# A top-one routed feed-forward stage: from all experts on all tokens to tiles of tokens sorted by expert

## The chip, the cores and the metric

The kernel runs on 1 core of one Trainium2 chip. The metric is the device time of a run in microseconds; shown is the median of three runs.

## What is computed

Eight residual stages in a row on x of 4 x 512 tokens of 128 features, all in f32. Each stage is `x = x + f(layernorm(x))`. The change is to the fourth, a routed feed-forward of 8 experts with 256 hidden features each, of which every token uses one, and a shared expert that every token uses:

```python
logits = x_ @ router.T
idx = jnp.argmax(logits, axis=-1)
onehot = jax.nn.one_hot(idx, router.shape[0], dtype=x.dtype)
u = jnp.einsum('bc,ehc->ebh', x_, up)
g = jnp.einsum('bc,ehc->ebh', x_, gate)
h = jax.nn.silu(g) * u
ye = jnp.einsum('ebh,ech->ebc', h, down)
y = jnp.einsum('ebc,be->bc', ye, onehot)
ys = jax.nn.silu(x_ @ w_gate_s.T) * (x_ @ w_up_s.T) @ w_down_s.T
```

The second stage is of the same kind with 16 experts of 64 features, four of them used by a token. The last one has 8 experts of 512 features, two used by a token, with a limit on the tokens of an expert.

## The kernel before

x stays in SBUF from the first stage to the last (`x_resid`, 16 tiles of 128 tokens). `program` (L2999) runs the stages one after the other; each is a block with an order of its own for every engine, and all engines meet at its end. Two weight buffers (`wbuf`) alternate: `load_next` (L132) clears the semaphores of the stage before last and has SP load the next stage's weights during the present one.

The second and the fourth stage are both `routed_ffn` (L1139). It takes 4 groups of 512 tokens. For each it normalizes (`LayerNorm`: statistics and scaling on VectorE, L190 to L201, the power on GpSimd, L225, turns on TensorE, L235, copies on ScalarE, L247 and L251), makes logits (L1239) and, from the ranks of the scores (`route_top1`, L1084), a matrix of weights per token and expert, zero where an expert isn't chosen. Then it goes through units of 128 hidden features, 18 a group in the fourth stage: 2 of the shared expert and 16 of the experts. `gate_up` (L1242) makes the gate and up products of all 512 tokens in three matmuls each, since operands are split into a high and a low part (fp32r) made by ScalarE and GpSimd, and a product that spreads the expert's weight over the unit's rows (L1263). ScalarE does SiLU (L1354) and the high part of the hidden values (L1338), VectorE two products (L1408, L1411), GpSimd the low part (L1227). `down` (L1277) adds the unit's share to the output, three units later (`LAG`). At the end of a group the output is turned back (L1297) and added to x (L1379). In all, 72 units.

The last stage, `dispatched_ffn` (L2641), isn't changed, but has the same steps as the new code. It chooses experts per 512 tokens, counts with triangular and all-ones matmuls how many tokens ahead chose the same expert (L2796 to L2801), makes a row number for each token and choice (L2913), and GpSimd scatters rows of 129 numbers (128 features and the token's own number) into a DRAM buffer with one indirect DMA per 128 rows (L2757). SP reads the rows expert by expert (L2730), TensorE turns them (L2818), multiplies them in f32 (L2827, L2837), GpSimd scatters results by token (L2772), SP reads them back (L2736) and VectorE adds them to x (L2992). The fields of that buffer are cleared ahead, in the sixth stage (L1465, L1467).

## Time and profile before

| what | us |
| --- | --- |
| median of three runs | 1818.81 (1815.47 to 1820.68) |
| profiled execution, from its first to its last instruction | 1817.4 |
| TensorE busy in it (matmuls) | 1503.1 (83%) |
| VectorE | 1168.3 (64%) |
| ScalarE | 819.9 (45%) |
| GpSimd | 813.0 (45%) |
| the fourth stage, from 564.7 to 762.5: TensorE busy | 184.35 of 197.80 |

The profile is of one execution, of which only the span is known, and that is the time it is read against. Matmuls are pipelined and the ends of their records are modelled, so a row's length is more than its beat. "Busy" leaves out register, semaphore and DMA-issuing instructions. PEclk is the granted TensorE clock as a share of full speed (2.4 GHz): 0.50 is 1.2 GHz. In a row of the timeline, "[idle before <-releaser]" is how long the engine waited and for what.

### The profile page before, as it was taken

How to read it: one execution, taken by the hardware profiler on the slowest of the kernel's cores; microseconds unless marked ns; L12 is line 12 of the kernel's file. 1: busy time of each engine (PE TensorE's matmuls, PEld its weight loads, DVE VectorE, ACT ScalarE, POOL GpSimd, SP SyncE). 2: the span in 40 equal slices, each digit the busy share in tenths (PEclk: the TensorE clock that was granted, in tenths of full speed). 3: DMA queues.
4: the chain of work that ended last, by engine and by line, in shares of the span. 5: the costliest groups of instructions: out<-in, count | busy, mean ns of one | idle time of the engine just before them, and what ended most of it. 6: DMA issues, size and time to landing. Idle time of an engine off the chain costs nothing. (4 is left out here: it accounts for less than half of the span.)

```text
span 1817.4 us, 25752 instructions
## 1 busy us (share of the span) xinstructions
PE 1503.1 (83%) x9316; PEld 932.3 (51%) x9316; DVE 1168.3 (64%) x2949; ACT 819.9 (45%) x1276; POOL 813.0 (45%) x847
## 2 busy tenths in 40 slices
PE   5576677889997999769997889979999999986194
PEld 2355555544444677534443567754555554544063
DVE  5766688568884766678885332257877877675302
ACT  3544333336664554355664433345545545450041
POOL 5451344612223855562323254235546556463633
PEclk9687699759997999858999899989999999998597
DMA  2000000100000000210000102000000000002113
GB/s 90 7 7 2 32 0 1 79 1 1 1 1 23 1 1 1 81 51 1 1 1 1 38 11 94 1 1 1 1 1 1 1 1 1 1 1 109 60 53 93
DMA packets 21597, 38.66 MB, mean 21 GB/s; under 512 B 2016, under 2 KB 18400, under 8 KB 20320
## 3 DMA queue, kind: packets, MB, share of 16 engines
q1 hardware_dynamic: 19424, 32.81, 5.2%
q0 software_dynamic: 2048, 4.21, 0.7%
q8 instruction: 75, 1.23, 0.3%
q14 instruction: 50, 0.41, 0.1%
HBM read 26.50 MB, written 9.47 MB: 20 GB/s over the span
## 5 line engine op out<-in xcount | busy, mean ns | idle before, releaser
L1982 DVE CUSTOM_DVE_ANT_0 s_masked_scores<-s_for_max,s_mask_qk 128x128 bf16<-128x128 f32 (+3 forms) x512 | 227.0, 486 | 58.9 <-PE s_for_max L1806 56.9
L2415 POOL TENSOR_TENSOR wbuf<-s_probs 128x1024 f32<-128x1024 f32 x64 | 151.9, 2374 | 206.6 <-ACT s_probs L2574 206.6
L2574 ACT ACTIVATE s_probs<-s_scores 128x1024 f32<-128x1024 f32 x128 | 132.2, 1033 | 201.7 <-PE s_scores L2496 201.7
L1758 POOL TENSOR_SCALAR_AFFINE_SELECT s_probs<-s_probs 128x256 f32<-128x256 f32 x256 | 100.9, 406 | 269.2 <-ACT s_probs L1913 156.1
L1227 POOL TENSOR_TENSOR s_hidden_lo<-s_hidden,s_hidden_hi 128x512 fp32r<-128x512 f32 x108 | 142.6, 1321 | 122.0 <-ACT s_hidden_hi L1338 121.9
L2616 DVE TENSOR_REDUCE s_negmax<-s_for_max 128x2 f32<-128x1024 f32 x126 | 152.2, 1208 | 20.1 <-PE s_for_max L2471 20.0
L1806 PE MATMUL s_for_max<-s_k_stack,s_q_stack 32*128 32x128 f32 (+3 forms) x512 | 142.2, 441 | 27.1 <-DVE s_max_wide L1982 17.4
L2623 DVE RECIPROCAL s_recip<-s_pv_and_sums 128x128 f32<-128x128 f32 x128 | 116.7, 934 | 47.3 <-PE s_pv_and_sums L2522 47.3
L1806 PEld LDWEIGHTS s_for_max<-s_k_stack,s_q_stack 32*128 32x128 f32 x512 | 72.0, 204 | 129.4 <-DVE s_max_wide L1982 88.5
L1913 ACT ACTIVATE s_probs<-s_scores 128x1024 f32<-128x1024 f32 x128 | 127.3, 1024 | 17.1 <-PE s_scores L1827 17.0
L2509 PE MATMUL s_pv_and_sums<-s_probs,s_v 128*64 128x512 f32 x512 | 123.9, 605 | 0.9 <-DVE wbuf L2631 0.9
L1354 ACT ACTIVATE s_silu<-s_gate 128x512 f32<-128x512 f32 x108 | 64.5, 598 | 120.4 <-PE s_comb L1263 111.2
L1408 DVE TENSOR_TENSOR s_gated<-s_silu,s_up 128x512 f32<-128x512 f32 x96 | 65.9, 687 | 61.4 <-ACT s_silu L1354 60.5
L1900 ACT ACTIVATE s_low_rows_hi<-s_odd_jobs,s_low_rows_bias,s_low_rows 128x512 fp32r<-128x512 f32 x64 | 49.8, 777 | 102.9 <-PE s_odd_jobs L1786 102.1
L1841 PE MATMUL s_pv<-s_probs,s_v_and_one 128*32 128x512 f32 (+3 forms) x1024 | 94.2, 462 | 1.5 <-DVE s_o L2001 1.5
L1827 PE MATMUL s_scores<-s_q_stack,s_k_stack 32*128 32x512 f32 (+3 forms) x512 | 82.0, 396 | 0.7 <-ACT s_probs L1913 0.7
L2420 POOL TENSOR_TENSOR xnT<-wbuf 128x1024 f32<-128x1024 f32 x32 | 78.1, 2440 | 2.5
L1338 ACT CAST s_hidden_hi<-s_hidden 128x512 fp32r<-128x512 f32 x108 | 66.2, 613 | 22.0 <-DVE s_hidden L1411 21.9
L1489 POOL TENSOR_TENSOR s_h_lo<-s_h,s_h_hi 128x512 fp32r<-128x512 f32 x32 | 42.5, 1330 | 71.0 <-DVE s_h_hi L1583 71.0
L2496 PE MATMUL s_scores<-s_q_hi,s_k_hi 64*128 64x512 f32 x256 | 63.8, 494 | 9.6 <-ACT s_probs L2574 9.6
L1411 DVE TENSOR_TENSOR s_hidden<-s_gated,s_comb 128x512 f32<-128x512 f32 x96 | 65.9, 687 | 3.3
L1288 PE MATMUL s_yT<-s_hidden_hi,s_w_hi 128*128 128x512 f32 x108 | 61.0, 565 | 3.6 <-POOL s_hidden_lo L1227 3.6
(490 smaller groups left out, 3768.5 us busy)
## 6 DMA issues: line engine op xcount, KB each, us to landing
s_w<-extra SPq DMA_DIRECT2D x2, 2048.0 KB, 10.2
wbuf<-w SPq DMA_DIRECT2D x1, 3460.0 KB, 11.2
s_probs<-extra SPq DMA_DIRECT2D x1, 2898.0 KB, 9.7
wbuf<-w SPq DMA_DIRECT2D x1, 2888.0 KB, 15.2
wbuf<-w SPq DMA_DIRECT2D x1, 2124.0 KB, 8.3
dispatched<-s_empty_slots SPq DMA_DIRECT2D x1, 2064.0 KB, 6.6
s_rows<-dispatched SPq DMA_DIRECT2D x8, 258.0 KB
expert_rows<-s_empty_slots SPq DMA_DIRECT2D x1, 2048.0 KB, 14.7
```

Source lines behind the costliest of these rows:

```text
L1227: nc.gpsimd.tensor_tensor(hid_lo[:, n % DEEP, :], hidden[:, n % DEEP, :], hid_hi[:, n % DEEP, :].bitcast(F32), ALU.subtract).then_inc(s_lo, 1)
L1758: last = nc.gpsimd.affine_select(out=diag, in_=diag, compare_op=ALU.is_ge, fill=0.0, base=0, pattern=[[0, diag.shape[1]], [1, P]], channel ...
L1806: last = nc.tensor.matmul(p1[m % 2][:, at:at + n], stacks[0][rows, q % SLOTS, i * P:n], stacks[1][rows, q % SLOTS, 0:n], start=True, stop= ...
L1827: last = nc.tensor.matmul(p2[n % 2][:, at:at + S - j * P], stacks[1][rows, q % SLOTS, j * P:(j + 1) * P], stacks[0][rows, q % SLOTS, j * P ...
L1841: last = nc.tensor.matmul(po[32 * x:32 * x + 32, j * P:S], v32[:, c % 2, j, 4 * g + x, :], probs[:, q % 2, slab, at:at + S - j * P], start ...
L1913: nc.scalar.activation(probs[:, q % 2, r, :], p2[n % 2][:, :], ACT.Exp, scale=scale).then_inc(s_exp, 1)
L1982: last = nc.vector.tensor_tensor_reduce(out=junk[:, m % 2, at:at + n], in0=p1[m % 2][:, at:at + n], in1=mask[:, S - n:S], scale=1.0, scala ...
L2415: nc.gpsimd.tensor_tensor(added[half], probs[:, g % 2, 2 * half, :, :], probs[:, g % 2, 2 * half + 1, :, :], ALU.add).then_inc(s_added, 1)
L2509: last = nc.tensor.matmul(po[x * dh:(x + 1) * dh, :], v[:, c % 2, j, (2 * n + x) * dh:(2 * n + x + 1) * dh], probs[:, g % 2, j, x, :], sta ...
L2574: nc.scalar.activation(probs[:, g % 2, j, :, :], p2[:, :, :], ACT.Exp, scale=dh ** -0.5).then_inc(s_exp, 1)
L2616: nc.vector.tensor_reduce(negmax[:, g % 2, :, j], max_bank(g, j)[:, :, :], AX.X, ALU.max, negate=True).then_inc(s_neg, 1)
L2623: nc.vector.reciprocal(recip[:, at], ps_sum[:, at]).then_inc(s_rec, 1)
```

## The change

The fourth stage becomes a function of its own, `sorted_ffn`, and `route_top1` and its steps are gone. It finds the expert of each token, counts the tokens of each expert, and gives each token a row in a DRAM buffer in which expert e starts at row 2048 e. From the counts it makes a table of 23 tiles of 128 rows (16 would do for full ones; each of 8 experts can end in a part-filled tile): the first row of each tile and the place of its expert's weights. SP reads the first row numbers into registers and loads the tiles; TensorE reads the places into registers and uses them as addresses of the moving operand. The last column of a row is its token, or 1000000 where the field is empty; the result of an empty row goes to a spare row. Matmuls are in plain f32, with no split. Weights are laid out expert by expert. The buffer's fields are filled in the second stage.

```diff
+SORT_TILES = T // P + 7
+SORT_ROWS = 8 * T + 1024
+SORT_CLEARS = 9
+NO_TOKEN = 1.0e6
```

In `routed_ffn`, for the run of it that comes before (a stage 3 follows):

```diff
         def _(sp):
             sh.load_next(sp, stage)
+            if clear:
+                sp.wait_ge(s_empty, 2)
+                for at in range(0, SORT_ROWS, T):
+                    n = min(T, SORT_ROWS - at) // P
+                    sp.dma_start(sh.by_expert[at:at + n * P].rearrange("(p r) d -> p r d", p=P),
+                                 empty[:, 0:n, :]).then_inc(sh.fields_cleared, 16)
+                sp.wait_ge(sh.fields_cleared, 16 * SORT_CLEARS)
...
                     split.gpsimd(pool, range(3 * block_no, 3 * block_no + 3))
+                if n == units and clear:
+                    nc.gpsimd.memset(empty[:, :, 0:D], 0.0).then_inc(s_empty, 1)
+                    nc.gpsimd.memset(empty[:, :, D], NO_TOKEN).then_inc(s_empty, 1)
                 pool.wait_ge(s_hi, n + 1)
```

The new stage, engine by engine (J = 23, RING = 6, WIDE = 768 columns of weights an expert; the increments of semaphores are mostly left out):

```python
def _(sp):
    sh.load_next(sp, stage)
    sp.wait_ge(s_table, 1)
    _, at = nc.values_load_multi_w_load_instructions(table_i[0:1, 1, :], ...)
    sp.wait_ge(s_put, 16 * NT)
    for j in range(J):
        if j >= RING:
            sp.wait_ge(s_turn, j - RING + 1)
            sp.wait_ge(s_placed, j - RING + 1)
        sp.dma_start(rows[:, j % RING, :], sh.by_expert[bass.ds(at[j], P), :])
    sp.wait_ge(s_out, 16 * J)
    for c in range(B):
        sp.dma_start(back[:, tiles(c), :], ...)

def _(pool):
...
    pool.wait_ge(sh.fields_cleared, 16 * SORT_CLEARS)
    for c in range(B):
        pool.wait_ge(s_idx, c + 1)
        for t in range(c * TPC, (c + 1) * TPC):
            nc.gpsimd.indirect_dma_start(sh.by_expert, ...idx[:, t:t + 1]..., xn[:, t, :], None)
    for j in range(J):
        pool.wait_ge(s_placed, j + 1)
        pool.wait_ge(s_y, j + 1)
        nc.gpsimd.indirect_dma_start(sh.by_token, ...place_i[:, j:j + 1]..., y[:, j, :], None)

def _(pe):
...
    def shared_up(c, f):
        pe.wait_ge(ln.ready, c + 1)
        if c:
            pe.wait_ge(s_hid, (c - 1) * n_sh + f + 1)
        for m, ps in zip(("gate", "up"), (ps_gu, ps_h)[f]):
            last = nc.tensor.matmul(ps[:, :], w[m][:, f * P:(f + 1) * P], sh.xnT[:, cols(c)], start=True, stop=True)
...
    for c in range(2):
        ln.turned(pe, c)
        logits(c)
    count(0)
    shared_up(0, 0)
    pe.wait_ge(s_chosen, 1)
    ln.turned(pe, 2)
    logits(2)
    count(1)
    shared_up(0, 1)
    pe.wait_ge(s_chosen, 2)
    ln.turned(pe, 3)
    logits(3)
    count(2)
    shared_up(1, 0)
    count(3)
    shared_down(0)
    shared_up(1, 1)
    shared_down(1)
    for c in range(2, B):
        for f in range(n_sh):
            shared_up(c, f)
        shared_down(c)
    pe.wait_ge(s_table, 1)
    _, at = nc.values_load_multi_w_load_instructions(table_i[0:1, 0, :], ...)

    def gate_up(j):
        pe.wait_ge(s_rowsT, j + 1)
        pe.wait_ge(*((s_hide, j - 1) if j >= 2 else (s_hid, B * n_sh)))
        nc.tensor.matmul(ps_gu[j % 2][:, :], rowsT[:, j % 3, :], w["experts"][:, bass.ds(at[j], 2 * f_exp)],
                         start=True, stop=True).then_inc(s_gu, 1)
...
    def down(j):
        pe.wait_ge(s_hidT, j + 1)
...
        for f in range(n_f):
            w_f = w["experts"][:, 2 * f_exp + f * P:]
            last = nc.tensor.matmul(ps_out[j % 2][:, 0:D], hidT[:, j % 2, f * P:(f + 1) * P],
                                    w_f[:, bass.ds(at[j], D)], start=(f == 0), stop=(f == n_f - 1))
...
    turn(0)
    turn(1)
    for j in range(J + 2):
        if j < J:
            gate_up(j)
        if j + 2 < J:
            turn(j + 2)
        if j >= 2:
            down(j - 2)
        if 1 <= j <= J:
            turn_hidden(j - 1)

def _(act):
...
    for j in range(J + 2):
        if j < J:
            act.wait_ge(s_gu, j + 1)
            nc.scalar.activation(silu_e[:, j % 2, :], ps_gu[j % 2][:, 0:f_exp], ACT.Silu)
        if j + 2 < J:
            take_rows(j + 2)
        if j >= 2:
            act.wait_ge(s_down, j - 1)
            nc.scalar.copy(y[:, j - 2, :], ps_out[j % 2][:, 0:D])

def _(dve):
...
    for j in range(J + 1):
        if j < J:
            dve.wait_ge(s_rows[j % RING], 16 * (j // RING + 1))
            nc.vector.tensor_tensor(place_i[:, j:j + 1], rows[:, j % RING, D:D + 1], spare[:, j:j + 1], ALU.min)
            dve.wait_ge(s_esilu, j + 1)
            if j >= 2:
                dve.wait_ge(s_hturn, j - 1)
            nc.vector.tensor_tensor(hid_e[:, j % 2, :], silu_e[:, j % 2, :], ps_gu[j % 2][:, f_exp:], ALU.mult)
        if j >= 1:
            dve.wait_ge(s_hturn, j)
            if j >= 3:
                dve.wait_ge(s_down, j - 2)
            nc.vector.tensor_copy(hidT[:, (j - 1) % 2, :], ps_h[(j - 1) % 2][:, 0:f_exp])
    for c in range(B):
        dve.wait_ge(s_back[c], 16)
        nc.vector.tensor_tensor(sh.x[:, tiles(c), :], sh.x[:, tiles(c), :], back[:, tiles(c), :], ALU.add)
```

VectorE's part ahead of these loops chooses the expert of a group of 512 tokens in five small operations, gives rows in five more, and after the fourth group makes the table in twelve; the shared expert's products stand in between, two of them ahead of the table.

## Rows read from the trace of the kernel before

**Rows 1.** The page's head.

```profile
span 1817.4 us, 25752 instructions
```

**Rows 2.** Windows, fourth stage: from:to, length, busy us (instructions) of each engine, PEclk, DMA share, GB/s.

```profile
564.70:762.50 197.80, 184.35 (x792) 136.21 (x792) 129.51 (x238) 97.96 (x190) 119.22 (x113) 0.95 0.02 6
```

**Rows 3.** Windows, two stretches of the fourth stage; columns as in rows 2.

```profile
582.00:591.00 9.00, 9.00 (x36) 7.71 (x36) 1.55 (x3) 4.42 (x9) 2.20 (x4) 0.50 0.01 2
591.00:757.50 166.50, 163.66 (x716) 119.99 (x714) 112.80 (x173) 86.29 (x166) 104.35 (x90) 1.00 0.00 1
```

**Rows 4.** Timeline, fourth stage: start us, length us, engine, line, operation, out<-in, count.

```profile
751.10 0.39 PE L1254 MATMUL s_gate<-s_xnT_hi,s_w_hi 128*128 128x512 f32 x1
...
753.42 0.39 PE L1254 MATMUL s_gate<-s_xnT_hi,s_w_hi 128*128 128x512 f32 x1
...
761.68 0.69 DVE L1379 TENSOR_TENSOR x_resid<-x_resid,s_route 128x512 f32<-128x512 f32 x1 [4.39 <-PE s_route L1297]
...
762.66 0.13 POOL L1727 IOTA s_row_number<- 128x1 int32 x1 [3.37 <-POOLq L1152]
```

**Rows 5.** Timeline, second stage: GpSimd's tenth low part, and the last addition.

```profile
264.72 1.29 POOL L1227 TENSOR_TENSOR s_hidden_lo<-s_hidden,s_hidden_hi 128x512 fp32r<-128x512 f32 x1 [1.15 <-ACT s_hidden_hi L1338]
...
341.74 0.69 DVE L1379 TENSOR_TENSOR x_resid<-x_resid,s_route 128x512 f32<-128x512 f32 x1 [4.39 <-PE s_route L1297]
```

**Rows 6.** DMA issues: out<-in, engine, count, KB each, median us to landing.

```profile
expert_rows<-s_empty_slots SPq DMA_DIRECT2D x1, 2048.0 KB, 14.7
...
wbuf<-w SPq DMA_DIRECT2D x1, 20.0 KB, 1.7
```

**Rows 7.** Timeline, last stage: statistics, first and last indices, last scatter, read, turn.

```profile
1661.72 0.87 DVE L190 BATCH_NORM_STATS2 s_ln_stats<-x_resid 128x6 f32<-128x128 f32 x4 [0.32 <-PEq L2314]
...
1675.36 0.17 DVE L2913 CAST s_idx<-s_where 128x4 uint32<-128x4 f32 x1
...
1695.14 0.17 DVE L2913 CAST s_idx<-s_where 128x4 uint32<-128x4 f32 x1
...
1719.69 0.96 POOL L2757 DMA_INDIRECT dispatched<-s_xn,s_idx  x1 [0.30 <-issue]
...
1721.97 44.16 SPq L2730 DMA_DIRECT2D s_rows<-dispatched  x8
...
1724.80 1.12 PE L2818 MATMUL s_turned<-ident,s_rows 128*128 128x128 f32 x4 [31.30 <-DMA s_rows<-dispatched]
```

**Rows 8.** Groups by line, last stage: busy us, mean ns of one, idle before.

```profile
L2865 ACT COPY s_rowsT<-s_turned 128x512 f32<-128x512 f32 x8 | 4.6, 578 | 36.2 <-PE s_turned L2818 36.2
...
L307 DVE TENSOR_REDUCE s_rank<-s_gt 128x32 f32<-128x256 f32 x4 | 1.7, 420 | 0.1
```

**Rows 9.** Timeline, last stage, TensorE in the first and third expert.

```profile
1726.69 5.96 PE L2827 MATMUL s_up<-s_rowsT,s_w 128*128 128x512 f32 x8 [0.77 <-ACT s_rowsT L2865]
...
1741.63 3.79 PE L2827 MATMUL s_up<-s_rowsT,s_w 128*128 128x512 f32 x8
...
1745.25 0.60 PE L2818 MATMUL s_turned<-ident,s_rows 128*128 128x128 f32 x4
...
1745.69 3.74 PE L2837 MATMUL s_y<-s_w,s_hidden 128*128 128x128 f32 x32
```

**Rows 10.** SP's semaphore clears: ns min/median/max, first and last start.

```profile
L136 SPq EVENT_SEMAPHORE_RANGE_CLEAR  x277: 25/30/49, 203.9 to 1663.6; - x139
```

**Rows 11.** Timeline, end of the last stage: last scatter, reads back, additions.

```profile
1797.47 0.95 POOL L2772 DMA_INDIRECT expert_rows<-s_y,s_place_int  x1 [0.30 <-issue]
1799.76 5.52 SPq L2736 DMA_DIRECT2D s_back<-expert_rows  x8
1802.61 2.19 DVE L2992 SCALAR_TENSOR_TENSOR x_resid<-s_back,s_gate,x_resid 128x128 f32<-128x128 f32 x8 [11.16 <-DMA s_back<-expert_rows]
1805.33 6.39 DVE L2992 SCALAR_TENSOR_TENSOR x_resid<-s_back,s_gate,x_resid 128x128 f32<-128x128 f32 x24 [0.53 <-DMA s_back<-expert_rows]
```

**Rows 12.** Windows, third stage; columns as in rows 2.

```profile
355.00:395.00 40.00, 31.26 (x99) 18.13 (x99) 24.32 (x89) 11.12 (x14) 12.71 (x16) 0.50 0.00 0
```

More of the change, by code:

```diff
@@ L1191, in routed_ffn @@
         s_down, s_yT, s_turned, s_x = sem("down_done"), sem("yT_copied"), sem("y_turned"), sem("x_updated")
+        clear = 3 in sh.weights
+        if clear:
+            empty = sb("empty_rows", [P, NT, D + 1])
+        s_empty = sem("empty_rows_made")
         block = ctx.enter_context(nc.Block())
@@ L3038 @@
     1: lambda sh, s: routed_ffn(sh, s, 16, 64, 128, ACT.Sigmoid, route_groups, ROUTE_GROUPS_STEPS),
[L3039 removed]
+    3: sorted_ffn,
     2: low_rank_attention,
@@ L3096, in _layout @@
     if stage == 3:
[L3097 to L3099 removed]
+        experts = [part for e in range(8) for part in (_t(a["gate"][e]), _t(a["up"][e]), _fold(_t(a["down"][e])))]
+        return [("router", _t(a["router"])), ("gate", _t(a["w_gate_s"])), ("up", _t(a["w_up_s"])),
+                ("down", _fold(_t(a["w_down_s"]))), ("experts", cat(*experts))]
     if stage == 4:
```

291 lines of the change are left out of this document (281 added, 10 removed).

## The prediction

> **What bounds it now.** I read the page's head first, for the span [rows 1], then the busy times by stage. The top-one stage (the second `routed_ffn`) holds 197.8 us, and TensorE is busy for 184.4 of them [rows 2]. Cut further, the stage has a cool start and then 166.5 us at full granted clock with TensorE busy for 163.7 [rows 3]. The timeline shows the beat: one unit (128 hidden columns of one expert for 512 tokens) every 2.32 us [rows 4]. There are 4 x 18 units: 16 of each 18 belong to experts, and each token uses only 2 of those 16. So it is bound by TensorE, by multiplying all tokens with all experts. The stage ends with the addition into x at 762.4, and the next one starts at 762.66 [rows 4].
>
> **The change, part by part.** Its model stands in the same trace: the last stage also counts places, scatters rows through DRAM, runs experts on them and takes the rows back.
>
> *Clears, in the first routed stage.* POOL fills 2064 columns and SP stores 17408 rows of 516 B, 8.98 MB. The fill goes in ahead of the tenth low part; that one starts at 264.7, and the last addition of that stage is at 341.7 [rows 5]. POOL rests a microsecond between low parts, and TensorE takes each three units later, so a 2 us delay is covered; uncovered it would cost 2 us. The nearest store is the second clear of the last stage's fields, landed 14.7 us after its issue, behind an equal one [rows 6]: 4.1 MB in 14.7 us, so 9 MB take about 32 us. There is room for 73 us; I count nothing.
>
> *Routing.* In the last stage, 33.6 us pass from the first statistics (1661.7) to the last indices (1695.3), 13.8 of them to the first [rows 7]. Here each 512 tokens need 10 small VectorE operations rather than 22, but in between TensorE turns tokens, makes logits and runs three shared gate/up pairs at the low clock. The two about cancel: I keep 33.6, between 28 (no shared pairs in the way) and 38. The table's twelve operations (0.2 to 0.4 us each [rows 8]) take 3.2 us, beside TensorE's shared work.
>
> *Scatter.* POOL issues one 128-row scatter every 1.26 us; 2.3 us after the last starts, SP issues the read, and TensorE has rows 2.8 us later [rows 7]. Of the 16 scatters, only the last four lie behind the last indices: rows are there 33.6 + 4 x 1.26 + 1.3 + 2.8 = 43 us after the start. TensorE is not ready by then (next), so they cost nothing; were it ready, this would be the gate. The 23 reads run six tiles ahead.
>
> *Shared expert.* Behind the last indices, TensorE still has five gate/up pairs and four down groups. In f32 a matmul makes two records; eight records of 512 columns take 3.79 us and 32 of 128 columns 3.74 us, at full clock [rows 9]. A pair (4 records) is then 1.9 us and a down group (16) 1.87. With three waits for SiLU and product of about 1.5 us: 5 x 1.9 + 4 x 1.87 + 4.5 = 21.5 us at full clock, 38.5 at the low one. In the trace TensorE ran 9.0 of 9.0 us at the low clock (582 to 591) before it rose [rows 3]; I take 27.
>
> *Register loads.* TensorE and SP each load 23 numbers from SBUF, in one call; TensorE does so after the shared work, with all tiles queued behind. No row shows a load. Lowest bound: 23 sequencer steps of 30 ns like the semaphore clears [rows 10], 0.7 us. Highest: 23 round trips like the 20 KB load, 1.7 us each [rows 6], 39 us. I take 4 us: a few round trips, since one call takes the whole list. SP's start once the table is ready and are 20 us ahead of TensorE's. The Trainium skill ("Runtime: NRT & Kernel Launch", The ~15µs preamble/postamble breakdown) gives about 1.3 us for a TENSOR_LOAD, a round trip to HBM for a few words; if each number is one, that would be 30 us on TensorE, if the list is one, near 1.3. No row here decides.
>
> *23 tiles.* Per tile TensorE does gate/up (2 records of 512 columns, 0.95 us), a turn (0.15), a down (4 of 128, 0.47) and two hidden turns (0.30) [rows 9]: 1.87 us at full clock, 3.7 at the low one. ScalarE: SiLU of 256 and two copies of 128, about 0.95, from 0.58 for 512 [rows 8]. VectorE: two operations of 256 at 0.42 and a small one, 1.0 [rows 8]. POOL: 1.26. TensorE is longest; each of its waits is for something made an interval earlier. I take 2.0 us a tile: 0.8 to fill, 46, and 2.9 until the last output is copied. Register addresses add sequencer work that no row prices: nothing (hidden behind array work) to a round trip each (a rival below).
>
> *End.* From the last scatter's start (1797.5) to SP's issue 2.3 us; first group 2.85 us later, third by 1805.3 [rows 11], so the fourth about 6.6 us after the issue; then an addition of 0.69, and 0.3 to the next stage.
>
> *Next stages.* The same 3460 KB of weights, in another order; SP has a few dozen more semaphores to clear at 30 ns. Nothing.
>
> **Sum**, from 564.7: 33.6 + 27 + 4 + 0.8 + 46 + 2.9 + 2.3 + 6.6 + 0.7 + 0.3 = 124.2 us, so the next stage starts at 688.9 rather than 762.7. That is 73.8 us less: 1817.4 - 73.8 = 1743.6 of span. The median of the runs, 1818.81, stands 1.4 above this span: forecast **1745 us**.
>
> **Rivals.**
> *A. One load, one round trip.* 39 us rather than 4: 1780. For it: 23 registers have to be filled somehow, and the only rows of a fetch are whole transfers. Against: nothing says that a fetch of a few words costs a transfer, or that loads go one by one. Chance 0.16.
> *B. TensorE stays at the low clock through the tiles.* For it: between 355 and 395 it was busy for 31.3 of 40 us and the clock stayed at 0.50, which is 1.2 GHz [rows 12]; while the registers load it is idle. Against: at that clock the tiles need 3.7 us each and leave no idle time, and in the last stage, after over 30 idle microseconds, it was at 0.47 us a record from the third expert on [rows 9]. Price (3.7 - 2.0) x 23 = 39: 1784. Chance 0.14.
> *C. The chain within a tile sets the beat.* Gate/up, SiLU, product, turns, copy, down are 3.5 us with their hand-overs, and only two buffers stand between them. At 3.0 us a tile: +23, 1768. For it: ten hand-overs a tile. Against: each wait is a full interval old. Chance 0.11.
> *D. Register addresses, and it gets slower.* Six records a tile have one: 138. If each holds the sequencer for a round trip of 1.7 us [rows 6], TensorE waits 138 x 1.7 = 235 us in place of hiding it: 1980. It decides from 73.8 / 138 = 0.53 us each. For it: no row shows one. Against: an address is arithmetic on a register already loaded, and the sequencer steps that the trace shows take 30 ns [rows 10]. Chance 0.03. The Trainium skill ("TensorE: Matmul & The Clock Gate", Decode and dispatch) puts the sequencer's handling of a MATMUL at about 62 ns where it decodes in microcode; for 138 that is 9 us, which would leave the gain; no row here shows it apart.
> *E. It doesn't do what it says:* the clears are not done by the end of the first routed stage. SP waits for all nine there, and every engine waits for SP. Up to 73 us (0.12 MB in a microsecond) they hide; from there each microsecond is one of the total, and at 146 us the gain is gone. Against: the two clears of [rows 6] moved 4.1 MB in 14.7 us, 0.28 in a microsecond, and would have to be more than four times as slow. Chance 0.02.
> The forecast with its own spread (1728 to 1762) has 0.54.
>
> **Numbers.** Range: below, the tiles at 1.87, shared work at 21.5 and loads at 0.7 give 1745 - 3 - 5.5 - 3.3 = 1733, and with the routing at 28, 1728; above it takes in C, A and most of B: **1728 to 1790**, leaving out D, E, and A with B. Faster by over 0.3% (5.5 us, about what a measurement here can tell): all but D and E and a mix of A, B and C at their worst: 0.94. Within 0.3%: 0.01, since the cases leave that stretch all but empty. Slower: 0.05.
>
> **What would show it.** The next stage's first row near 689. Timeline: last indices near 598, gate/up of the first tile near 630, then one every 2.0 us. TensorE's idle time ahead of the first turn, put down to issue, is the register load: 4 us right, 30 or more A. The granted clock over the tiles: 1.00 right, 0.50 B. If it is 1.00 and gate/up waits for ScalarE or VectorE, C; if TensorE idles on issue before each register-addressed matmul, D. In the first routed stage the end should stay at 341.7, else E. The forecast is wrong if TensorE is not the engine that the tiles wait for, or if first rows arrive after the shared work ends.

## Result and profile after

The changed kernel takes 1725.19 us (median of 4 runs, 1719.87 to 1726.45) against 1818.73 (4 runs, 1815.47 to 1820.68) for the kernel before: a ratio of 0.9474, 95% interval 0.9453 to 0.9495. The forecast was 1745, range 1728 to 1790: the direction was right, but the gain is 94 us where 74 were expected, and the time lies 2.8 us below the range. The same program was timed nine times more on other occasions; its 13 runs reach from 1719.87 to 1734.50, with the median at 1729.14. (e3 below came out as the same program too, with 1732.13; it isn't among the 13.) One program thus spreads over 15 us. Part of that is the moment at which the stage starts, part are waits that come and go; both are followed up below.

The span is 1723.9 us (1817.4 before). Nearly all of the difference lies in the top-one stage, which now goes from 565.95 to 666.90, 101.0 us, against 198.0 before [rows 2, 4]: 97.0 less. Of that, 1.2 are lost ahead of it, since it starts later, and 2.3 behind it. The busy times by stretches (routing, rest of the shared expert, tiles, end):

```profile
core 0: us, PE busy (x) PEld busy (x) DVE busy (x) ACT busy (x) POOL busy (x), PEclk, DMA share, GB/s
566.00:594.00 28.00, 21.79 (x103) 14.25 (x104) 17.06 (x93) 5.41 (x8) 16.52 (x30) 0.63 0.17 58
594.00:616.20 22.20, 17.19 (x76) 10.92 (x74) 8.40 (x22) 2.98 (x5) 5.76 (x7) 0.92 0.14 40
616.60:655.00 38.40, 37.46 (x198) 24.46 (x199) 19.43 (x69) 18.11 (x67) 19.14 (x20) 1.00 0.22 63
657.40:666.90 9.50, 0.00 (x0) 0.00 (x0) 2.77 (x4) 0.03 (x1) 1.17 (x3) 0.50 0.44 124
```

In the tiles TensorE is busy for 37.46 of 38.40 us at full clock, as it was before [rows 3]: they are bound by TensorE. Ahead of them stand 50 us, and behind them 9.5, in which TensorE has pauses or nothing to do. The timeline of the transition and of the steady state:

```profile
593.64 0.35 DVE L1737 CAST s_idx<-s_where 128x4 uint32<-128x4 f32 x1
614.10 2.05 PE L1601 MATMUL s_ps_y<-wbuf,s_shared_hidden 128*128 128x128 f32 x16 [1.41 <-DVE s_shared_hidden L1763]
616.62 0.43 PE L1638 MATMUL s_ps_turned<-ident,s_rows 128*128 128x128 f32 x2 [0.46 <-issue]
617.36 1.12 PE L1643 MATMUL s_ps_gate_up<-wbuf,s_rowsT 128*128 x2 [0.32 <-ACT s_rowsT L1689]
...
626.47 1.02 PE L1643 MATMUL s_ps_gate_up<-wbuf,s_rowsT 128*128 x2
627.33 0.27 PE L1638 MATMUL s_ps_turned<-ident,s_rows 128*128 128x128 f32 x1
627.44 0.61 PE L1663 MATMUL s_ps_route<-wbuf,s_hiddenT 128*128 x4
627.88 0.38 PE L1651 MATMUL s_ps_hidden<-ident,s_hidden 128*128 128x128 f32 x2
628.10 1.02 PE L1643 MATMUL s_ps_gate_up<-wbuf,s_rowsT 128*128 x2
```

The last indices are there at 593.99; the first turn follows the last shared down group with only 0.46 us of "issue", which is all of the register load that is bare; from the fourth tile on there is a gate/up every 1.63 or 1.64 us, and up to the last one none of TensorE's rows has a wait. The register loads themselves, one instruction on each engine (the rows of their two lines):

```profile
L1513 SPq TENSOR_LOAD <-s_table_int x1: 5156/5156/5156, 596.8 to 596.8; - x1
L1631 PEldq TENSOR_LOAD <-s_table_int x1: 2281/2281/2281, 614.2 to 614.2; - x1
```

And the end, to be set beside that of the last stage [rows 11]:

```profile
657.17 0.27 ACT L1710 COPY s_y<-s_ps_route 128x128 f32<-128x128 f32 x1 [1.26 <-PE s_ps_route L1663]
658.19 0.96 POOL L1557 DMA_INDIRECT rows_by_token<-s_y,s_place_int  x1 [0.57 <-issue]
660.42 2.04 SPq L1524 DMA_DIRECT2D s_back<-rows_by_token  x4
663.24 0.69 DVE L1819 TENSOR_TENSOR x_resid<-x_resid,s_back 128x512 f32<-128x512 f32 x1 [6.96 <-DMA s_back<-rows_by_token]
664.22 0.69 DVE L1819 TENSOR_TENSOR x_resid<-x_resid,s_back 128x512 f32<-128x512 f32 x1 [0.28 <-DMA s_back<-rows_by_token]
665.11 1.48 DVE L1819 TENSOR_TENSOR x_resid<-x_resid,s_back 128x512 f32<-128x512 f32 x2 [0.20 <-DMA s_back<-rows_by_token]
666.90 0.13 POOL L2125 IOTA s_row_number<- 128x1 int32 x1 [7.75 <-POOLq L1452]
```

### The profile page after: what moved, and what is told of

The parts are those of the page before. It is cut to its first block and busy times, and to the rows that moved or that the text cites. A ratio compares the mean times of both kernels' runs of the same rounds, so it can differ in the third digit from the quotient of the medians.

```text
span 1723.9 us, 24914 instructions
## 1 busy us (share of the span) xinstructions
PE 1397.6 (81%) x8900; PEld 849.7 (49%) x8907; DVE 1088.7 (63%) x2898; ACT 749.2 (43%) x1168; POOL 741.1 (43%) x795
## 5 line engine op out<-in xcount | busy, mean ns | idle before, releaser
L2156 POOL TENSOR_SCALAR_AFFINE_SELECT s_probs<-s_probs 128x256 f32<-128x256 f32 x256 | 100.9, 407 | 269.6 <-ACT s_probs L2311 155.4
L2298 ACT ACTIVATE s_low_rows_hi<-s_odd_jobs,s_low_rows_bias,s_low_rows 128x512 fp32r<-128x512 f32 x64 | 49.7, 777 | 101.7 <-PE s_odd_jobs L2184 100.9
L1242 POOL TENSOR_TENSOR s_hidden_lo<-s_hidden,s_hidden_hi 128x512 fp32r<-128x512 f32 x36 | 49.4, 1372 | 56.2 <-ACT s_hidden_hi L1353 56.2
L2894 PEld LDWEIGHTS s_scores<-s_q_hi,s_k_hi 64*128 64x128 f32 x256 | 23.8, 183 | 77.2 <-issue 56.2
L2907 PEld LDWEIGHTS s_pv_and_sums<-s_probs,s_v 128*64 128x64 f32 x512 | 31.2, 136 | 61.4 <-issue 61.4
L2869 PE MATMUL s_for_max<-s_k_hi,s_q_hi 64*128 64x512 f32 x252 | 51.2, 401 | 1.6 <-DVE s_negmax L3014 0.8
L2894 PE MATMUL s_scores<-s_q_lo,s_k_hi 64*128 64x512 f32 x256 | 51.0, 393 | 0.0
L3170 POOL DMA_INDIRECT expert_rows<-s_y,s_place_int x32 | 30.6, 957 | 47.4 <-DVE s_place_int L3379 37.3
## 6 DMA issues: line engine op xcount, KB each, us to landing
s_probs<-extra SPq DMA_DIRECT2D x1, 2898.0 KB, 10.1
```

Source lines behind the costliest of these rows:

```text
L2156: last = nc.gpsimd.affine_select(out=diag, in_=diag, compare_op=ALU.is_ge, fill=0.0, base=0, pattern=[[0, diag.shape[1]], [1, P]], channel ...
L2894: last = nc.tensor.matmul(p2[:, x, :], kp, qp, start=(part == 0), stop=(part == 3))
L2907: last = nc.tensor.matmul(po[x * dh:(x + 1) * dh, :], v[:, c % 2, j, (2 * n + x) * dh:(2 * n + x + 1) * dh], probs[:, g % 2, j, x, :], sta ...
```

## The experiments

Theory: the stage is a sum of four pieces one behind the other (routing 28.0, rest of the shared expert 22.1 and the load's bare 0.5, tiles 40.8, end 9.5), and the tiles' piece is TensorE's array work at full clock. Rivals: register addresses or loads cost (A, D); a queue or the chain of rows stands behind TensorE (C); the clears cost. Since parts upstream start the stage anywhere between 564 and 575 us, from run to run and with the clock granted there, each profile is read from its own stage's start; a single total has that spread in it. This table is worked out from the timelines: from the stage's first POOL row to the end of the last indices, to the first gate/up of a tile, from that to the last gate/up, and the stage's length.

| kernel | last indices | first gate/up | first to last gate/up | stage |
|---|---|---|---|---|
| changed, profile above | 28.0 | 51.4 | 35.2 | 101.0 |
| e11, e14: changed again | 30.2, 30.2 | 52.7, 52.8 | 35.2 | 102.5, 102.7 |
| e3: changed, as it came out | 27.4 | 57.7 | 35.2 | 107.6 |
| e1: 30 tiles | 27.6 | 52.6 | 46.7 | 113.9 |
| e2: fixed addresses | 30.2 | 52.0 | 35.1 | 101.7 |
| e4: no shared expert | 23.7 | 37.3 | 36.9 | 89.1 |
| e7: pairs late | 23.7 | 55.3 | 35.2 | 105.2 |
| e9: loads in halves | 28.1 | 51.6 | 35.2 | 101.2 |
| e6, e15: last group behind | 26.7, 30.2 | 50.7, 45.8 | 35.2 | 100.9, 96.1 |
| e8: both | 23.0 | 51.2 | 35.2 | 101.5 |
| e10: e6, plain stores | 30.2 | 45.8 | 35.2 | 96.1 |
| e12: warmed | 27.3 | 55.4 | 35.2 | 105.2 |
| e13, e16: warmed, plain stores | 20.8, 20.9 | 44.4, 44.3 | 35.2 | 94.2, 94.3 |
| e17: warmed, scatters paused | 20.8 | 44.5 | 35.2 | 94.1 |
| e18: e17, last group behind | 20.8 | 41.4 | 36.3 | 92.8 |

**The beat: 30 tiles.**

```
     J, WIDE, RING = SORT_TILES, 3 * f_exp, 6
+    EXTRA = 7
+    RUN_J, src = J + EXTRA, lambda j: max(j - EXTRA, 0)
...
-            for j in range(J + 2):
+            for j in range(RUN_J + 2):
```

> Tiles 0 to 6 are run twice, the first time without a scatter; the rest is as in the changed kernel, whose 23 tiles follow one another every 1.64 us with TensorE busy for nearly all of it. Theory (TensorE's array work sets the beat, at full clock): seven more tiles cost 7 x 1.64 = 11.4 us, total 1736.6, spacing of gate/up unchanged at 1.63 to 1.64. Rival (a queue behind the tiles, POOL's scatters at 1.26 us or SP's reads, has slack that is used up at the end): less than 1.64 a tile at the end, that is under 9 us more, since POOL would catch up. Rival (the clock falls when the tiles go on for longer): over 13 us more and a granted clock below 0.95 over the tiles.

The stretch from first to last gate/up grew from 35.16 to 46.67 us: 11.51 for seven tiles, 1.64 each, at a granted clock of 1.00. The seven tiles cost their full beat, so no queue behind TensorE had slack that could hide them. The total of this one run, 1743.45, is more than the 1736.6 expected: the stage started at 572.5 (6.6 us later, a stretch that the edit doesn't touch), and its shared work took 1.6 more.

**Register addresses: constants.**

```
- _, at = nc.values_load_multi_w_load_instructions(table_i[0:1, 0, :], engines=[mybir.EngineType.PE], ...)
+ at = [(j * n_exp // J) * WIDE for j in range(J)]
```

> TensorE's addresses are constants of the program (tile j takes expert j x 8 / 23), so its register load and its address steps are gone; some tiles are thus multiplied by another expert's weights. SP still loads and uses its registers. Theory (address arithmetic of 46 ns is hidden behind array work; of the 2.3 us load all but some 0.5 us lay beside the last shared down group): 0.5 us less at the most, 1724.7, tile spacing unchanged at 1.63. Rival D (register addresses hold the sequencer): spacing falls under 1.55, over 2 us less in the tiles. Rival A (the load is a path of its own): 2.3 us less.

35.08 us from first to last gate/up against 35.16, the same beat of 1.63 and 1.64. So D is out: with constants TensorE gains 0.08 us over 23 tiles. The stage took 101.7 us, beside 102.5 and 102.7 for the changed kernel with its indices at the same 30.2: 0.8 to 1.0 less. The total, 1734.2 where 1724.7 was expected, again carries a late start (572.8).

**Register loads: twice, and in halves.** The first was to double them and didn't:

> Both register loads are made twice in a row, on TensorE 23 numbers of 2.28 us, on SP 23 numbers of 5.16 us. Theory (TensorE's load ends 0.5 us after the shared work, SP's lies beside the scatters and the shared expert with over 8 us to spare): TensorE's second load is bare, 2.3 us more, SP's costs nothing: 1727.5. Rival (SP's load gates the first rows): 5.2 us or more on top of that, 1730 to 1732. Rival (a second load overlaps the first in the queue): under 1 us.

Of each pair the compiler dropped the first, whose numbers nobody used, and what ran was the changed kernel again (one load of 2.28 us on TensorE, one of 5.02 on SP). It told nothing of loads, but its tiles started 6.3 us later than in the profile above; that is followed up below. So the list was split:

```
- ... = nc.values_load_multi_w_load_instructions(table_i[0:1, 0, :], ...)
+ lists = [nc.values_load_multi_w_load_instructions(table_i[0:1, 0, a:b], ...)[1] for a, b in ((0, 12), (12, J))]
```

> Each register load, on TensorE and on SP, is made in two calls, of 12 and 11 numbers. Theory (the time goes by the count of numbers, about 0.1 us each on TensorE and 0.22 on SP): two loads of 1.2 and 1.1 us on TensorE, 2.7 and 2.5 on SP, tiles start as in the changed kernel. Rival (the time is that of a call, a round trip): two of 2.3 us on TensorE and two of 5.2 on SP, tiles start 2.3 us later. The case e3_loads_twice did not tell this, since the compiler dropped the first load of each pair as unused.

```profile
L1513 SPq TENSOR_LOAD <-s_table_int x2: 2286/2564/2843, 595.1 to 598.0; - x2
L1632 PEldq TENSOR_LOAD <-s_table_int x2: 1040/1184/1327, 612.5 to 613.6; - x2
```

On TensorE 1.33 and 1.04 us, together 2.37 where one call took 2.28; on SP 2.84 and 2.29, together 5.13 against 5.16. The time goes by the count of numbers, about 0.1 us each on TensorE and 0.22 on SP, and a further call costs 0.1 us on TensorE and nothing that can be seen on SP. Rival A, a round trip of 1.7 us for each number, is out, and so is one round trip for a list.

**No shared expert.**

```
 count(2)
-shared_up(1, 0)
 count(3)
-shared_down(0)
 ...
```

> The shared expert is left out of this stage: eight gate/up pairs, four down groups and their additions. In the changed kernel they hold TensorE for 22.1 us between the last indices and the first tile, and three pairs of about 9.5 us lie in the routing. Theory (behind them stands the chain of last scatters, register load of SP and first rows, which came some 11 us after the last indices): the first turn moves to 11 us after the last indices, and those come some 5 to 8 us earlier; the stage shrinks by 16 to 19 us, not by 31, total 1706 to 1709, if the clock is as high as before over the tiles. Rival (the chain is not a gate): 25 us or more less. Rival B (without the shared work TensorE comes to the tiles at the low clock and stays there): tiles every 2.9 to 3.3 us at 0.50, total 1735 or more.

The chain behind it showed itself (rows of VectorE, POOL, SP and TensorE):

```profile
596.24 0.17 DVE L1722 CAST s_idx<-s_where 128x4 uint32<-128x4 f32 x1
604.79 0.96 POOL L1552 DMA_INDIRECT rows_by_expert<-s_xn,s_idx  x1 [0.30 <-issue]
607.26 14.83 SPq L1521 DMA_DIRECT2D s_rows<-rows_by_expert  x13
609.02 0.48 PE L1628 MATMUL s_ps_turned<-ident,s_rows 128*128 128x128 f32 x1 [15.45 <-DMA s_rows<-rows_by_expert]
609.97 2.04 PE L1633 MATMUL s_ps_gate_up<-wbuf,s_rowsT 128*128 x2
```

The first turn comes 12.6 us after the last indices, 36.3 after the stage's start. POOL issues its 16 scatters without a pause from 585.61 on, one in 1.26 us: even the four groups' indices are ahead of it. So without the shared expert the gate is not "last indices + 11" but "first indices + 16 scatters + 2.5 + 1.8"; that is where the stage's start can go at best. The first gate/ups follow one another after 2.05, 1.98 and 1.95 us (the granted clock from 610 to 615 was 0.64, and 1.00 after that); against the profile above this is 1.8 us in all, which is what B amounts to here, not 39. The stage is 11.9 us shorter than in the profile above, and 13.5 than e11 and e14; 16 to 19 were expected. The total, 1723.2, is far from the 1706 to 1709 expected: the start at 572.7 is 6.8 us of it.

**The clears alone**, put into the kernel before.

> The kernel before with one part of the change, the POOL fill and the nine stores of the clears in the first routed stage; the top-one stage is as before. Theory (the fill delays one low part by under 1 us beside TensorE's work, the stores end long before the stage does): that stage's last addition at 341.7 to 342.5, total within 1 us of the kernel before. Rival (the 1.23 us by which the stage ended later in the changed kernel comes from the clears): 343.0, total 1.2 us more. Rival E (SP waits for the clears at the stage's end): a gap ahead of the next stage.

```profile
340.64 0.69 DVE L1399 TENSOR_TENSOR x_resid<-x_resid,s_route 128x512 f32<-128x512 f32 x1 [4.40 <-PE s_route L1317]
```

The addition that ends the first routed stage is at 340.64, against 341.74 in the kernel before [rows 5] and 342.97 in the changed one; the total was 1818.99 beside 1821.05. The same changed kernel had it at 345.44 in e14, and e9 at 340.92, so 1.2 us are within the spread of that moment. From its own first POOL row to that of the next stage, the first routed stage took 138.8 us before, 138.7 in e5 and 137.9 in the changed kernel: the clears cost nothing that can be seen.

**The place of the shared work.** Ahead of the tiles the last group costs its time in full, at the end TensorE idles for 9.5 us [last row of the first fence]. So move it:

```
-for c in range(2, B):
+for c in range(2, B - 1):
     ...
 ...
     if 1 <= j <= J:
         turn_hidden(j - 1)
+pe.wait_ge(s_hide, J)
+shared_up(B - 1, 0)
+pe.wait_ge(s_hidT, J)
+shared_up(B - 1, 1)
+pe.wait_ge(s_y, J)
+shared_down(B - 1)
```

> The shared expert of the last 512 tokens (two gate/up pairs, a down group, its addition) moves from ahead of the tiles to behind them, beside the last scatter and the read back, where TensorE has nothing for some 9 us in the changed kernel. Theory (the shared expert holds TensorE ahead of the tiles, and the first rows are there from about 41 us after the stage's start): tiles start 7 us earlier, since that group takes 1.88 + 1.88 + 1.41 + 2.05; behind them it takes some 8 us of the 9 free: total 7 us less than the changed kernel, about 1718. Rival (the chain of scatter, register load and first rows is as late as the shared expert): 2 us or less. Rival (behind the tiles TensorE falls to the low clock and the group runs past the read back): 3 to 4 us less.

It was 1723.53 (1722.03 to 1727.42, 4 runs), ratio 0.9465, interval 0.9445 to 0.9485: not to be told from the changed kernel, where 7 us less were expected. In its profile the 7 us were gained and lost again: ScalarE went on at 603.46 from a gate/up pair that TensorE had ended at 595.21. The two that shift the three pairs of the routing behind it, alone and with the last group behind the tiles:

> The three gate/up pairs that run within the routing wait until its last counts are issued; nothing else. The prediction kept 28 us as the routing's lower bound without these pairs. Theory: the last indices come at 20 to 22 us after the stage's start rather than 28, the shared work behind them grows by as much, tiles start within 2 us of 50.7 us. Rival (TensorE rises to the full clock later for want of work in the routing, so that more of the shared work is at the low clock): tiles start 3 to 5 us later.

> As e6_last_group_behind, and the three gate/up pairs that run within the routing wait until its last counts are issued. Theory (TensorE's work ahead of the tiles is only shifted, but the indices come 6 to 8 us earlier, so the rows can no longer be late, and more of the shared work falls at the low clock): within 2 us of e6_last_group_behind. Rival (the indices and their scatters are what the stage waits for): 4 us or more less than it.

e7 (1730.23, one run) had its last indices at 23.7 rather than 28.0, not at 20 to 22, and tiles 3.9 us later than the profile above, in the rival's range. e8 was 1729.39 (1722.63 to 1732.02), 5.9 more than e6 where within 2 were expected; the intervals of the two overlap (e8's ratio is 0.9487, 0.9459 to 0.9515). Earlier indices didn't help. In both, results of TensorE were taken up late as in e6: 6.3 us in e7, 6.5 in e8, at the worst. So the profile of e7 doesn't show that the clock, which the rival named, is the reason for its later tiles.

**The late hand-overs.** In e3, which is the same program as the changed kernel:

```profile
591.43 1.88 PE L1596 MATMUL s_ps_hidden<-xnT,wbuf 128*128 128x512 f32 x4
601.10 0.60 ACT L1689 ACTIVATE s_shared_silu<-s_ps_hidden 128x512 f32<-128x512 f32 x1 [11.73 <-remote]
603.16 3.75 PE L1604 MATMUL s_ps_y<-wbuf,s_shared_hidden 128*128 128x128 f32 x16 [9.85 <-DVE x_resid L1774]
```

The pair ends at 593.31; SiLU, which waits for nothing else, starts 7.8 us later, and the profile finds no releaser of this core ("remote"). Both engines were idle. While ScalarE waited, the clock fell: it was 0.50 from 601 to 606, and the down group that follows shows 3.75 us instead of 2.05. The kernel before has no such row in this stage, nor has the changed kernel's own profile; e1, e4, e6, e7 and e8 had late ones, e2 not. e9 had a short one, of 1.4 us (the group ends at 600.08, the addition starts at 601.45), and its stage was hardly longer for it (101.2):

```profile
597.02 3.06 PE L1602 MATMUL s_ps_y<-wbuf,s_shared_hidden 128*128 128x128 f32 x16 [2.15 <-DVE x_resid L1770]
601.45 0.69 DVE L1770 TENSOR_TENSOR x_resid<-x_resid,s_ps_y 128x512 f32<-128x512 f32 x1 [4.58 <-PE s_ps_y L1602]
```

A first guess was the clock, which rose early in e3 and e6. To separate it from the scatters and from the place in the program:

```
-    nc.gpsimd.indirect_dma_start(sh.by_expert, bass.IndirectOffsetOnAxis(ap=idx[:, t:t + 1], axis=0), xn[:, t, :], None)
+    (on SP) sp.dma_start(sh.by_expert[t * P:(t + 1) * P, :], xn[:, t, :]).then_inc(s_put, 16)
```

> On e6_last_group_behind: the 16 scatters by POOL become 16 plain stores by SP, of the same 128 rows each, to places fixed in the program, and the 23 reads take fixed places too; so the rows are not sorted, and most are multiplied by an expert that is not theirs. In e6_last_group_behind ScalarE went on 8.2 us after TensorE's pair of the second group had ended, at the moment when the scatters had drained, and the same was seen, from 2 to 8 us, in four other kernels. Theory (these waits belong to the scatters that POOL makes): no such wait here, the shared work between the last indices and the first tile takes some 15 us, tiles start 43 to 45 us after the stage's start, total about 1717. Rival (they belong to any stores beside the shared work, or to neither): waits of 2 us and more stay, tiles start at 48 us or later, total above 1721.

> The changed kernel again, on the same chip and beside the same runs of the kernel before as e10_plain_puts. Its own profile had no late hand-over, e3_loads_twice, which came out as the same program, had two of 2.1 and 7.8 us. Theory (they come and go from run to run with the moment at which TensorE's clock rises): total between 1718 and 1732; with a late hand-over when the clock rises before 584, none when it rises after 588. Rival (they come from the place of the instructions in the program): none in this profile, whatever the clock, total within 1720 to 1727.

Neither had a late one, and in both the indices came at 30.2 us, with TensorE at the low clock until then: so e10 said nothing yet about scatters, and e11, the program of e3, spoke against a fixed place. What they did tell, free of late hand-overs: tiles start at 45.8 against 52.7, 6.9 us earlier, and the stage is 6.4 shorter. e10 took 1721.99 us (1716.53 to 1728.37) where 1717 was expected, e11 1729.79 (1728.95 to 1732.60). Then the clock was raised on purpose:

```
+def busy(n):
+    for _ in range(n):
+        nc.tensor.matmul(ps_gu[0][:, :], sh.ident[:, :], w["experts"][:, 0:S], start=True, stop=True)
+busy(4)
 for c in range(2):
     ln.turned(pe, c)
+    busy(1)
     logits(c)
```

> The changed kernel with six more matmuls of 512 columns, whose result nobody reads: four ahead of the first turn of the stage, one behind each of the first two groups' turns, to bring TensorE to the full clock early in the routing. Theory (late hand-overs come when TensorE is at the full clock beside the scatters): the last indices come 3 to 6 us earlier, a hand-over of TensorE's result is 2 us or more late, up to 8, and the total is no better than the changed kernel's, 1720 to 1732. Rival (they are chance, or lie in the place of the code): none, tiles start at 45 us after the stage's start, total 5 us less than the changed kernel. Second rival (these matmuls do not raise the clock): all as in the changed kernel, 1 to 3 us later.

> e12_warm with POOL's 16 scatters replaced by 16 plain stores by SP to fixed places, and fixed places for the 23 reads, so that most rows are multiplied by an expert that is not theirs. Theory (the late hand-overs belong to POOL's scatters): none here at the full clock, tiles start at 43 to 46 us, total 5 us less than e12_warm or more. Rival (any stores beside TensorE's full clock do it): late hand-overs as in e12_warm, total within 2 us of it.

e12 took 1730.44 us (1727.34 to 1739.12; ratio 0.9525, interval 0.9499 to 0.9551), e13 1718.66 (1716.06 to 1722.55; 0.9441, 0.9426 to 0.9456), 11.8 less on one chip. Both had the clock at 1.00 from 570 to 590. The busy times of the eleven us behind, of e12:

```profile
590.00:601.00 11.00, 0.20 (x1) 0.00 (x0) 4.44 (x19) 0.60 (x1) 5.77 (x6) 0.61 0.13 42
```

and of e13:

```profile
590.00:601.00 11.00, 8.86 (x41) 6.08 (x41) 5.90 (x21) 0.73 (x2) 0.00 (x0) 0.84 0.29 76
```

TensorE, the first busy time, stood still in e12. The hand-overs in the timeline of e12:

```profile
586.35 0.24 PE L1584 MATMUL s_ps_route<-s_chosen,s_ones 128*128 128x8 bf16 x4
588.32 1.88 PE L1593 MATMUL s_ps_hidden<-xnT,wbuf 128*128 128x512 f32 x4
592.12 0.19 DVE L1738 TENSOR_TENSOR s_slot_of<-s_ps_route,s_numbers 128x32 f32<-128x32 f32 x1 [5.94 <-remote]
600.06 0.60 ACT L1689 ACTIVATE s_shared_silu<-s_ps_hidden 128x512 f32<-128x512 f32 x1 [12.33 <-remote]
```

and the same two of e13:

```profile
589.73 0.24 PE L1583 MATMUL s_ps_route<-s_chosen,s_ones 128*128 128x8 bf16 x4
590.00 0.19 DVE L1737 TENSOR_TENSOR s_slot_of<-s_ps_route,s_numbers 128x32 f32<-128x32 f32 x1 [0.45 <-PE s_ps_route L1583]
591.69 1.88 PE L1592 MATMUL s_ps_hidden<-xnT,wbuf 128*128 128x512 f32 x4
593.61 0.60 ACT L1688 ACTIVATE s_shared_silu<-s_ps_hidden 128x512 f32<-128x512 f32 x1 [3.48 <-PE s_ps_hidden L1592]
```

In e12 the counts of the last group end at 586.59 and are taken up at 592.12, 5.5 us late; the pair ends at 590.20 and is taken up at 600.06, 9.9 late. In e13 the same two follow within 0.04 us. Not all of the 11 us by which e12's stage is longer are waiting: the clock was 0.50 from 595 to 605 after TensorE had stood still, and its next down group shows 3.75 us. Is it POOL as the issuer, or the indirect form?

> e13_warm_plain_puts with the 16 plain stores to fixed places issued by POOL rather than SP (most rows are again multiplied by an expert that is not theirs). Theory (the indirect form is what goes with the late hand-overs, in which POOL works out a descriptor for each row for nearly 1 us a scatter): none here, the stage takes 94 to 95 us, total within 2 us of e13_warm_plain_puts. Rival (any store issued by POOL): hand-overs 2 us and more late, the stage takes 98 us or more.

No late hand-over, stage 94.3 us, 1719.85 (1718.33 to 1727.31). So POOL as the issuer is out, and what is left is what goes with the indirect form. That is more than one thing: e13 and e16 also write each group of rows to one place rather than to scattered ones, and SP has no registers to load in them. Which of these counts was not tested. The changed kernel and the one with the last group behind its tiles, side by side:

> The changed kernel, for comparison with e15_group_behind_again on the same chip: about 1725, between 1720 and 1732.

> The kernel of e6_last_group_behind again. Theory (of the 6.9 us that the last shared group takes ahead of the tiles 6.4 are gained where no hand-over is late, as e10_plain_puts against e11_changed_again showed): 3 to 6.5 us less than e14_changed_beside_e15, since some runs lose it again to late hand-overs. Rival (late hand-overs take all of it): within 2 us of it.

e14 was 1732.15 (1726.38 to 1734.50, 5 runs), ratio 0.9513, interval 0.9496 to 0.9531; e15 1728.63 (1717.60 to 1731.15, 6 runs), 0.9481, interval 0.9453 to 0.9509. That is 3.5 us less, with intervals that overlap a little; in the two profiles, both without late hand-overs, the stages are 102.7 and 96.1 us. Over all runs of each, 13 and 10, the medians are 1729.1 and 1725.5. The end of e15's stage:

```profile
660.21 1.88 PE L1593 MATMUL s_ps_gate_up<-xnT,wbuf 128*128 128x512 f32 x4
663.67 2.04 SPq L1524 DMA_DIRECT2D s_back<-rows_by_token  x4
665.26 2.02 PE L1601 MATMUL s_ps_y<-wbuf,s_shared_hidden 128*128 128x128 f32 x16 [1.46 <-issue]
667.32 0.69 DVE L1776 TENSOR_TENSOR x_resid<-x_resid,s_ps_y 128x512 f32<-128x512 f32 x1 [2.16 <-PE s_ps_y L1601]
668.04 2.50 DVE L1831 TENSOR_TENSOR x_resid<-x_resid,s_back 128x512 f32<-128x512 f32 x4
```

The group fits: its addition ends as the rows come back, and the four last additions then run without a wait. A second group there would be bare (not run), since TensorE is done at 667.3 and the rows are back by then.

**Clock or series.** Laid side by side, the profiles have a better divide than the clock. With the first three groups' indices 7 us apart POOL scatters four times and waits; where they come faster than it can scatter (4 x 1.26 = 5 us a group), the scatters run on unbroken. By the time that a hand-over late by over 0.6 us was taken up, six or more had been issued without a pause (by the end of TensorE's work it had been five at the least): at the full clock (e1, e3, e6, e12) and at the low one (e4, e7, e8); e9's came after eight. The reverse does not hold: the last two groups' indices always come close together, so e2, e9, e11, e14 and e15 have eight in a row too, and in e2, e11, e14 and e15 a SiLU with six of them issued was on time (e11: the pair ends at 603.82, SiLU starts at 603.86). The last two runs keep full clock, indirect scatters and fast routing, and break the series:

```
 pool.wait_ge(s_idx, c + 1)
+if c:
+    pool.wait_ge(s_put, 16 * TPC * c)
 for t in range(c * TPC, (c + 1) * TPC):
```

> e12_warm with one wait more: POOL begins a group's four scatters only when those of the groups before it have landed, so that no more than four follow one another. Full clock through the routing as in e12_warm, all of the computation as in the reference. Theory (late hand-overs come with an unbroken series of scatters): none late by over 0.6 us, last indices at 21 us, first rows at 41 to 42 us by 4 groups of 4 x 1.26 + 2.3, just ahead of TensorE at 44; stage 94 to 95 us, total 8 to 11 us under e12_warm, about 1719. Rival (they come with the full clock beside indirect scatters): late by 2 us and more as in e12_warm, total within 3 us of it.

> e17_warm_paused with the last group's shared work behind the tiles, as in e6_last_group_behind. TensorE would be ready for the tiles at 37.5 us, the rows are there at 41 to 42. Theory: first gate/up at 42 to 43 us, stage 92 to 93 us, 1.5 to 2 us under e17_warm_paused, total about 1717. Rival (rows that come later than TensorE is ready let its clock fall): stage 95 us or more.

e17 took 1720.32 us (1717.46 to 1727.57, 6 runs), ratio 0.9449, interval 0.9426 to 0.9473, and e18 1719.22 (1714.00 to 1723.60, 5 runs), 0.9443, interval 0.9421 to 0.9466. In e17 the granted clock was 1.00 up to 590. Its hand-overs, and POOL's pause at 592:

```profile
586.90 0.19 DVE L1740 TENSOR_TENSOR s_slot_of<-s_ps_route,s_numbers 128x32 f32<-128x32 f32 x1 [0.45 <-PE s_ps_route L1586]
589.28 0.96 POOL L1554 DMA_INDIRECT rows_by_expert<-s_xn,s_idx  x1 [0.30 <-issue]
590.50 0.60 ACT L1691 ACTIVATE s_shared_silu<-s_ps_hidden 128x512 f32<-128x512 f32 x1 [3.48 <-PE s_ps_hidden L1595]
592.32 0.96 POOL L1554 DMA_INDIRECT rows_by_expert<-s_xn,s_idx  x1 [2.08 <-DMA rows_by_expert<-s_xn,s_idx]
605.42 9.93 SPq L1521 DMA_DIRECT2D s_rows<-rows_by_expert  x9
610.66 0.42 PE L1646 MATMUL s_ps_turned<-ident,s_rows 128*128 128x128 f32 x2 [0.47 <-issue]
```

Every result is taken up within 0.04 us of its end once the scatters have begun. The stage took 94.1 us against 105.2 for e12, from which it differs by that one wait; the last scatter starts 4.6 us later and still nobody waits for it. The totals, taken on two chips, are 10.1 us apart, with intervals that don't overlap. In e18 the rows do gate: TensorE waits 4.1 us for them, its first tiles take 1.2 us longer than in e17, and the stage is 1.3 us shorter still, 92.8; the medians of the two are 1.1 apart, which the runs can't tell. Both keep all of the computation. Against e11 and e14, whose hand-overs were on time too, e17's stage is 8.5 us shorter, its last indices 9.4 us earlier; e12 had the same clock and lost all of that to the late hand-overs. e18's stage is 8 to 15 us shorter than the changed kernel's in its four profiles, and its median 10 us under the 1729.1 of all 13 runs; its interval lies below e11's and e14's and overlaps the first one's (from 0.9453) a little.

## Why the prediction was wrong in its sizes and right in its mechanism

Its structure held: TensorE bound the stage before and binds the tiles now, at full clock; POOL, ScalarE and VectorE have slack; the scatters, the fill, the clears and SP's load are hidden. The time did not: it came out 20 us under the forecast and below the range. The sum was 124.2 us from 564.7 and is 101.0 from 565.95. By its terms:

- *Tiles, 46 + 0.8 + 2.9 = 49.7; measured 40.8 from the first turn to the last copy.* **This is the step that failed**, by 9 us. The text adds 0.95, 0.15, 0.47 and 0.30 to "1.87 us at full clock" and takes 2.0: it took busy lengths of rows for beats. The same group of rows had the beat in it: eight records in 3.79 us are 0.474 each [rows 9], but that length holds the modelled end of the last; starts follow one another every 0.43 (two pairs of four records, 609.09 and 610.81 in the changed kernel, are 1.72 apart, with rows of 1.88). The section ahead of the prediction had said itself that a row's length is more than its beat. A tile by beats, from start to start in the rows above (626.47 to 628.10), is 0.86 + 0.11 + 0.44 + 0.22 = 1.63, and that is what ran. And there are no waits to add: each hand-over is an interval old, as the text itself said, so the addition of 0.13 a tile had no row behind it.
- *Shared work, 27; measured 22.1.* The step put part of this work at the low clock, by the cool start that the stage had before [rows 3]. Here the routing keeps TensorE busy (21.79 of 28 us), the clock is up before it ends, and over the shared work it was 0.92. The lower bound, 21.5, was the better guess; its parts (1.88, 1.88, a wait of 1.41, 2.05 for a group) were right to 0.2.
- *Routing, 33.6; measured 28.0,* and 27.3 to 30.2 in other profiles with pairs in it: at the lower bound that had been kept for "no shared pairs in the way". Shorter choices and longer TensorE work did not cancel.
- *Register load, 4; measured 2.28, of which 0.46 bare.* It runs on TensorE's queue beside the last down group's array work, which the step did not consider. The size was off as well. The Trainium skill ("Runtime: NRT & Kernel Launch", Instruction fetch mechanics) also gives about 200 ns for each register even in a bulk load, an estimate of 4.6 us by its figure. The runs agree on SP (0.22 us each) and show half of it on TensorE (0.10).
- *End, 2.3 + 6.6 + 0.7 + 0.3 = 9.9 and the last scatter; measured 9.46 from the last copy to the next stage.* Right.
- *Clears, next stages: nothing.* Right for the clears, by e5. From the next stage's first row to the end of the span it is 1054.7 us in the kernel before, 1057.0 in the profile above, 1055.6 in e14 and 1055.7 in e11: about 1 to 2 us more, which no run explains. *Scatters: nothing,* because rows would be there before TensorE is ready. That was right for the chain of rows, and for the profile above. But beside an unbroken series of scatters TensorE's results can be held up: 6.6 us of the stage in e3, against the profile above, and 11 in e12 (105.2 against 94.1). No row of the kernel before could show this price.

Together: 9 for the tiles, 5 for the shared work, 6 for the routing and 3.5 for the load are the 23 us between 124.2 and 101.0; the later start and the stages behind gave 3.5 of them back. All four misses have one sign, since each unknown was taken on its dear side or between ends; the range's lower end, 1728, took them one by one and kept the beat at 1.87. Of the rivals, A and D fell to e9 and e2, C to the profile above and e1 (no wait in the beat), E to e5; of B there are 1.8 us in the first tiles, and only without the shared expert (e4). None of them foresaw the late hand-overs.

## What to carry to other kernels

Take a beat from the distance between starts of equal rows, never from the length of a merged row over its count, and add no allowance for waits that are an interval old. In a stage whose main loop is at its limit, count what stands ahead of and behind the loop on the same engine; work that feeds nothing in the loop belongs where the engine waits for the last transfer. Where a long series of indirect stores runs beside matmuls whose results are waited for, look for late hand-overs and try to break the series (here: four, then wait until they have landed; this was run only with the clock raised early, not on the changed kernel as it stands). Read such a kernel from more than one profile.

## What the runs showed of the hardware that was not expected

- **Results of TensorE are taken up late beside an unbroken series of POOL's indirect scatters.** Up to 9.9 us, in e1, e3, e4, e6, e7, e8 and e12, and 1.4 us in e9; not with plain stores by SP or POOL (e10, e13, e16), nor with scatters in fours (e17, e18), all at the full clock but e10. In e3 and e6 the wait ended when the series had drained (SP's first row read, which waits for it, is issued at 600.83 and ScalarE goes on at 601.10; 602.88 and 603.46 in e6), in e8 and e12 some ended earlier. Length alone is not the rule: the changed kernel's own profile has eight in a row from the end of its routing on and a shared down group that ends at 601.84 and is taken up at 601.87, and e2, e11, e14 and e15 have eight in a row and nothing late. Whether TensorE's last records or its signal are held, no row shows; nor was the unbroken issue told apart from the number of rows on their way, since the wait in e17 changes both. That stays open.
- **Loads of registers are priced by the number, differently by engine:** 0.10 us each on TensorE, 0.22 on SP, and TensorE's goes on beside its array's work. A register-addressed matmul costs next to nothing beside array work (0.08 us over 138 records, e2).
- **The same stage starts 564 to 575 us after the kernel's start,** and that goes for the most part with the granted clock in the stage before (0.50 from 550 to 562 in e14, 1.00 in the profile above); more than any of the smaller edits moves.
